# Attention and routing stage of an adaLN + mixture-of-experts block: statistics and normalised rows computed a step further ahead, one product moved to GpSimd, two extra matmuls per step

## The chip, the cores and the metric

One NeuronCore of a Trainium2 chip runs the whole program. The metric is the device time of one execution in microseconds (us); the median of three runs is quoted, and one further execution was profiled.

## The reference, cut to what matters

```python
# x: 16 batches x 512 tokens x 256; c: 16 x 256
mod = (silu(c) @ wmod).reshape(16, 6, 1, 256)           # sa, ca, ga, sb, cb, gb; ga, gb kept away from 0
h = layernorm(x) * (1 + ca) + sa
q, k, v = phi(h @ W_q), phi(h @ W_k), h @ W_v           # 64 wide, phi = elu + 1
o = causal linear attention: (sum_{s<=t} (q_t . k_s) v_s) / max(q_t . sum_{s<=t} k_s, 1e-6)
x = x + ga * (o @ W_o)
h = layernorm(x) * (1 + cb) + sb
logits = layernorm(h; rn_g, rn_b) @ router_w.T + router_b   # 8 experts, top 2, softmax
x = x + gb * sum over the 2 experts of weight * ffn_e(layernorm(h; ln_g[e], ln_b[e]))   # 256 -> 1024 -> 256, gelu
```

## The kernel before, in words

The program is written with an instruction stream per engine and semaphores between them; nothing reorders it. It has three parts. A short setup loads constants and computes `mod`. Then an attention and routing stage (to about 380 us) handles the 16 batches of 512 tokens. Last, an expert stage (380 us to the end) runs 71 tiles of up to 256 tokens through the expert networks. The change touches only the setup and the attention stage.

The attention stage is a software pipeline. `pipeline` calls `step(i, ...)` for i = 0 to 20 on every engine, and within one step the engines work on different batches, chosen by six flags: `project` (batch i, for i under 16), `attend` (batch i-1), `settle` (i-2), `norm` (i-3), `route` (i-4) and `place` (i-5). `r` is the parity of i. In one step:

- SP (the DMA queue) loads x two batches ahead (`load_x`, L366), stores finished rows, and loads the modulation rows `gaB` and `csB`. It also streams the expert weights in, which are split into two bf16 parts on the way.
- DVE (`step`, from L864 on) takes the mean and variance of the three layer norms: of x of batch i+1 (`stats(rows(i + 1), 0)`, bn_stats, L771), of the attention's result of batch i-2 (form 1), and of the modulated rows `h2` of batch i-3 (form 2). `moments` is L779, `var_eps` writes `ve` (L786).
- POOL turns `ve` into the inverse root `rs` with a power (`inverse_root`, L544), once a step for the three norms together, then DVE forms `nm` = -mean * rs (L803). `nm_s` counts them.
- ACT applies `rs` and `nm` (`normalise`, L628): to x at the start of the next step (`xc`), to the attention's result (`xn2`), and to `h2` (`nrm`).
- DVE modulates: `h2 = xn2 * csB` (L901), then `h2 += csB` (L908), both 128 partitions x 1024 elements.
- PE transposes `xc` (L1322), computes the scores of batch i-1 (L1334), the ranks of batch i-5 (L1341 to L1345), the projections of batch i (L1355 to L1358), the transposes of `nrm` (L1369), the product with k (L1381 to L1387), logits (L1398), the output projection (L1407) and transposes of k (L1414). In odd steps four matmuls for a bias (L1315) come first. The scores use the banks that the output projection filled, so they wait until DVE has added them to x (`x2`, L968).
- DVE forms phi(q), phi(k) (L926), running sums and the denominator (L930, L932), the low parts of the expert weights (L940 in odd steps, L946 in even ones), then `den`, the residual sum `x2` (L968), the choice of experts (`choose`, `dl`, `ix`, `oh`, `ohs`), and with PE's ranks the list positions `slot` (`cnt`, `pick`, `slotf`, L1046 to L1064).
- POOL forms `wog` (L559, 64 x 256), and sends each batch's 512 rows to the experts' lists by 8 indirect DMAs (L551), four before the power (`scatter(.., (0, 1))`, waiting for `slot`), four behind it.

```python
                if place:                                            # POOL, L560 on
                    ...
                    scatter(i - 5, 1 - r, (0, 1))
                if project or attend or norm:
                    inverse_root(i + 1, 1 - r)
                if place:
                    scatter(i - 5, 1 - r, (2, 3))
```

## Time and profile before

| | |
|---|---|
| median of 3 runs | 1125.11 us (1123.71 to 1125.61) |
| the profiled execution, its own time | 1125.48 us |
| its span, first to last instruction | 1123.6 us |
| mean granted TensorE clock | 0.922 of full |
| busy over the span: PE, DVE, ACT, POOL | 88%, 79%, 48%, 51% |
| in 140 to 300 us: PE, DVE, ACT, POOL (busy us of 160) | 131.2, 151.2, 128.4, 104.3 |
| granted clock, 100 to 300 us / 420 us to the end | 0.81 to 0.89 / 1.00 |

A row of the profile names an engine, a source line, an operation, what it writes and reads (out<-in by the program's names), and its times. "store" is a large buffer that holds x, weights and several tiles; "banks" is PSUM. A busy engine is one that executes; waiting and the issue of plain DMAs are not counted. In the stage to 380 us PE is not at its full clock all the time; in the expert stage it is.

### The profile page before, as it was taken

The page shows a single profiled execution, that of the slowest core. Times are in us where ns is not written, and L with a number is a line of the kernel's source. Part 1 is how long each engine was busy: PE and PEld are TensorE (multiplying, and loading weights), DVE is VectorE, ACT ScalarE, POOL GpSimd, SP SyncE. Part 2 cuts the span into 40 slices and gives each one's busy share as a digit, 9 for nine tenths or more (in the row PEclk, how much of TensorE's full clock was granted, in tenths as well). Part 3 has the DMA queues.
Part 4 walks back from the last instruction along what each step waited for, and adds up shares of the span by engine and source line. Part 5 has one row for each costly group of instructions (what it writes and reads, how often), then busy time and mean ns, then how long its engine had stood idle before and what let it go on. Part 6 is the DMA issues. An engine that isn't in the chain of part 4 may idle for free.

```text
span 1123.6 us, 31567 instructions
## 1 busy us (share of the span) xinstructions
PE 988.9 (88%) x8116; PEld 806.3 (72%) x8117; DVE 889.1 (79%) x3010; ACT 542.9 (48%) x1123; POOL 573.6 (51%) x478
## 2 busy tenths in 40 slices
PE   5777879887945099999999999999999999999997
PEld 1334545554534088888888888888888888888875
DVE  5578999999985567777877877877877877877776
ACT  1668787878843134434444443444443443444443
POOL 2121666666667536655455445445445445545543
PEclk8798888888965599999999999999999999999999
DMA  4465777876869466665565555566555556566453
GB/s 134 133 227 194 237 230 260 291 271 212 315 233 401 122 185 132 137 123 92 96 118 98 106 112 104 98 109 99 94 108 103 90 108 108 87 120 122 88 100 49
DMA packets 162626, 169.80 MB, mean 151 GB/s; under 512 B 89340, under 2 KB 136968, under 8 KB 158472
## 3 DMA queue, kind: packets, MB, share of 16 engines
q1 hardware_dynamic: 129736, 114.24, 36.5%
q0 software_dynamic: 32832, 54.88, 25.3%
q8 instruction: 25, 0.41, 0.2%
q14 instruction: 33, 0.27, 0.1%
HBM read 94.67 MB, written 62.78 MB: 140 GB/s over the span
## 4 chain that ended last, share of the span: by engine, by line
PE 66%; issue 8%; DVE 8%; POOL 6%; ACT 2%; DMA 1%; POOLq 0%; DVEq 0%; SPq 0%; ACTq 0%
PE banks L1440 32%; PE banks L1452 31%; POOL lists L551 5%; PE banks L1334 2%; DVE st L771 2%; POOL rs L544 2%; DVE store L968 1%; PE banks L1322 1%; ACT rowbuf L628 1%; DVE mv L779 1%; ACT store L712 1%; DVE rowbuf L908 1%; DMA out<-rowbuf,ydst 0%; DVE store L926 0%; DVE ix L1001 0%
## 5 line engine op out<-in xcount | busy, mean ns | idle before, releaser
L1440 PE MATMUL banks<-nhl,store 128*128 128x256 bf16 (+1 forms) x3408 | 450.5, 268 | 28.0 <-DMA nhl<-xhl 24.8
L740 ACT ACTIVATE gf<-banks,b1t 128x256 f32<-128x256 f32 (+1 forms) x568 | 263.0, 463 | 429.1 <-PE banks L1440 411.7
L1452 PE MATMUL banks<-store 128*128 x3240 | 448.0, 273 | 0.5
L1440 PEld LDWEIGHTS banks<-nhl,store 128*128 x3408 | 324.1, 98 | 71.0 <-issue 30.1
L587 POOL DMA_INDIRECT out<-rowbuf,ydst x135 | 223.7, 1657 | 294.1 <-DVE rowbuf L1222 222.0
L1452 PEld LDWEIGHTS banks<-store 128*128 128x128 bf16 x3240 | 310.5, 98 | 41.9 <-issue 1.8
L1231 DVE CAST store<-gf 128x256 bf16<-128x256 f32 (+1 forms) x568 | 180.5, 318 | 130.7 <-ACT gf L740 99.3
L1233 DVE TENSOR_TENSOR store<-gf,store 128x256 bf16<-128x256 f32 (+1 forms) x568 | 234.7, 413 | 19.5
L551 POOL DMA_INDIRECT lists<-store,slot x128 | 141.0, 1102 | 96.3 <-issue 49.0
L578 POOL DMA_INDIRECT store<-y_rows,ygb x135 | 135.2, 1001 | 63.3 <-issue 51.8
L544 POOL TENSOR_TENSOR rs<-ve,mhalf 128x12 f32<-128x12 f32 (+2 forms) x20 | 39.0, 1950 | 84.6 <-DVE ve L786 84.5
L628 ACT ACTIVATE rowbuf<-store,nm,rs 128x256 f32<-128x256 f32 x128 | 66.1, 588 | 23.5 <-DVE nm L803 23.3
L1222 DVE SCALAR_TENSOR_TENSOR rowbuf<-rowbuf,yw,store 128x256 f32<-128x256 f32 x135 | 59.4, 479 | 0.2 <-DVE rowbuf L1212 0.2
L1322 PE MATMUL banks<-ident,rowbuf 128*128 128x128 f32 x128 | 25.1, 360 | 31.8 <-ACT rowbuf L628 31.8
L1334 PE MATMUL banks<-store,vT 64*128 64x512 f32 (+3 forms) x128 | 38.4, 662 | 16.5 <-DVE store L968 8.5
L1183 DVE TENSOR_TENSOR xhl<-rowbuf,xhl 128x512 bf16<-128x512 f32 (+1 forms) x71 | 46.6, 658 | 7.7 <-ACT xhl L731 7.7
L731 ACT ACTIVATE xhl<-rowbuf 128x512 bf16<-128x512 f32 (+1 forms) x71 | 42.6, 600 | 18.4 <-DMA rowbuf<-lists 18.4
L1212 DVE TENSOR_TENSOR rowbuf<-banks,b2t 128x256 f32<-128x256 f32 x135 | 50.8, 416 | 0.7 <-PE banks L1452 0.7
L1322 PEld LDWEIGHTS banks<-ident,rowbuf 128*128 128x128 f32 x128 | 19.7, 183 | 41.1 <-ACT rowbuf L628 39.5
L771 DVE BATCH_NORM_STATS2 st<-store 128x6 f32<-128x256 f32 x128 | 44.8, 412 | 2.3 <-DMA store<-in_L_attn_x 2.0
L1355 PE MATMUL banks<-store,wqk 128*128 128x512 f32 x64 | 42.0, 790 | 3.0 <-ACT store L664 3.0
L1334 PEld LDWEIGHTS banks<-store,vT 64*128 64x128 f32 x128 | 23.2, 276 | 27.6 <-issue 24.5
(225 smaller groups left out, 970.0 us busy)
## 6 DMA issues: line engine op xcount, KB each, us to landing
rowbuf<-lists SPq DMA_DIRECT2D x64, 264.0 KB
store<-in_L_ffn_w SPq DMA_DIRECT2D x16, 1024.0 KB, 6.0
wsplit<-store SPq DMA_DIRECT2D x16, 1024.0 KB, 5.7
store<-wsplit SPq DMA_DIRECT2D x16, 1024.0 KB, 11.1
b2t<-in_L_ffn_b SPq DMA_DIRECT2D x71, 128.0 KB
store<-in_L_attn_x SPq DMA_DIRECT2D x16, 512.0 KB, 9.6
out<-store SPq DMA_DIRECT2D x16, 512.0 KB, 9.9
csB<-mod_rows SPq DMA_DIRECT2D x16, 256.0 KB, 4.0
```

What stands on the lines that cost most here:

```text
L544: g.tensor_tensor(rs[:, r, n, :], ve[:, n, :], mhalf[:, n, :], ALU.pow).then_inc(rs_s, 1)
L551: g.indirect_dma_start(list_d, bass.IndirectOffsetOnAxis(ap=slot[:, b % NR, t, c:c + 1], axis=0), nrm[:, b % NR, c, :], None).then_inc(sca ...
L578: g.indirect_dma_start(gbr[:, r, h, :], None, y_d[GBROW:GBROW + NB, :], bass.IndirectOffsetOnAxis(ap=ygb[:, r, h:h + 1], axis=0)).then_inc ...
L587: g.indirect_dma_start(out_rows, bass.IndirectOffsetOnAxis(ap=ydst[:, r, h:h + 1], axis=0), yt[:, r, h, :], None, compute_op=ALU.add).then ...
L628: last = a.activation(out(c), src(c), ACT.Identity, bias=nm[:, r, n, c:c + 1], scale=rs[:, r, n, c:c + 1])
L740: a.activation(gf[:, c % 2, 0:halves(j) * P], MM[c % 2][:, 0:halves(j) * P], ACT.Gelu, bias=b1t[:, r, c:c + 1]).then_inc(gf_s, 1)
L771: last = v.bn_stats(st[:, n, c, :], src(c))
L1231: v.tensor_copy(gh[:, c, cols], gf[:, c % 2, cols]).then_inc(gh_s, 1)
L1233: v.tensor_tensor(gl[:, c, cols], gf[:, c % 2, cols], gh[:, c, cols], ALU.subtract).then_inc(gl_s, 1)
L1334: last = t.matmul(SC[s], vT[at, q, s // 2 * P:(s // 2 + 1) * P], q_of[at, q, s * P:T], start=True, stop=True)
L1440: last = t.matmul(MM[c % 2][:, 0:halves(j) * P], w, nhl[:, r, m, 0:halves(j) * P], start=n == 0, stop=n == 5)
L1452: last = t.matmul(ACC[r][h][:, 0:D], g[:, c, h * P:(h + 1) * P], w, start=c == 0 and n == 0, stop=c == NI - 1 and n == 2)
```

## The change

In the attention stage, the statistics of x are taken for batch i+2 in step i (batch 0 and 1 before the first step), and ACT normalises batch i+1 near the end of step i (`centred`) where it used to normalise batch i at the start of step i. Power and `nm` are still formed once a step, with one more before the first step. SP loads x of batches 2 and 3 in step 0 and i+3 in step i. The product `xn2 * csB` is done by POOL, behind `wog` and ahead of the first four scatter DMAs; DVE adds to its result. PE runs two matmuls on the constants `ident` and `onesf` into the bank `Q` ahead of the projections, which overwrite it. The sum for the router's bias moves from the setup to the end of DVE's step 0.

```diff
@@ SP @@
             def load_x(i, half, r):
-                if isinstance(i, int):
-                    if i + 2 < NB:
-                        sp.wait_ge(got_x[r], 16 * (half + 1))
-                        sp.dma_start(resid[:, (i + 2) * NC:(i + 3) * NC, :], x_v[i + 2]).then_inc(got_x[r], 16)
...
+                for b in range(2 if i == 0 else i + 3, min(i + 4, NB)):
+                    sp.wait_ge(got_x[b % 2], 16 * (b // 2))
+                    sp.dma_start(resid[:, b * NC:(b + 1) * NC, :], x_v[b]).then_inc(got_x[b % 2], 16)
@@ POOL @@
+            inverse_root(-1, 1)
             inverse_root(0, 0)
...
+                if norm:
+                    b, q = i - 3, 1 - r
+                    pool.wait_ge(got_cs[q], 16 * (half if q == 0 else half - 1))
+                    pool.wait_ge(xn2_s, b + 1)
+                    wait_past(pool, nrm_s, b - 1)
+                    g.tensor_tensor(h2[q], xn2, csB[:, q, D:2 * D].unsqueeze(1).to_broadcast([P, NC, D]), ALU.mult).then_inc(h2m_s, 1)
                 if place:
@@ ACT @@
+            def centred(b, r):
+
+                act.wait_ge(got_x[b % 2], 16 * (b // 2) + 16)
+                wait_past(act, xT_s, b)
+                normalise(lambda c: xc[:, c, :], rows(b), r, 0, xc_s)
+
+            act.wait_ge(nm_s, 1)
+            centred(0, 1)
...
-                if project or norm or route:
-                    act.wait_ge(nm_s, i + 1)
-                if project:
-                    act.wait_ge(got_x[r], 16 * half + 16)
-                    wait_past(act, xT_s, i)
-                    normalise(lambda c: xc[:, c, :], rows(i), r, 0, xc_s)
...
+                if 0 < i < NB - 1:
+                    centred(i + 1, r)
                 if project:
                     act.wait_ge(phi_s, i + 1)
@@ DVE @@
-            var_eps(0, 1)
+            var_eps(-1, 1)
+            dve.wait_ge(got_x[1], 16)
+            dve.wait_ge(mv_s, 1)
+            hold(dve, "dve")
+            stats(rows(1), 0)
+            neg_mean_rstd(-1, 1)
+            dve.wait_ge(nm_s, 1)
+            dve.wait_ge(ve_s, 1)
+            moments(0, 1)
+            var_eps(0, 2)
...
-                if project and not (isinstance(i, int) and i == NB - 1):
-                    if r == 0:
-                        dve.wait_ge(got_x[1], 16 * half + 16)
-                    else:
-                        dve.wait_ge(got_x[0], 16 * half + 32)
+                if i + 2 < NB:
+                    dve.wait_ge(got_x[r], 16 * half + 32)
                     hold(dve, "dve")
-                    stats(rows(i + 1), 0)
+                    stats(rows(i + 2), 0)
                 if norm:
...
-                    v.tensor_tensor(h2[q], xn2, csB[:, q, D:2 * D].unsqueeze(1).to_broadcast([P, NC, D]), ALU.mult).then_inc(h2m_s, 1)
+                    dve.wait_ge(h2m_s, b + 1)
+                    hold(dve, "dve")
+                    v.tensor_tensor(h2[q], h2[q], csB[:, q, 0:D].unsqueeze(1).to_broadcast([P, NC, D]), ALU.add).then_inc(h2_s, 1)
@@ PE @@
                 if project:
-                    pe.wait_ge(hT_s, i + 1)
                     if r == 0:
                         wait_past(pe, phi_s, i)
                     else:
                         pe.wait_ge(b1r_s, half + 1)
+                    if i == 0:
+                        pe.wait_ge(modc_s, 1)
+                    for n in range(2):
+                        t.matmul(Q[:, :], ident[:, :], onesf[:, :], start=True, stop=True)
+                    pe.wait_ge(hT_s, i + 1)
                     wait_past(pe, ktok_s, i)
```

POOL, one full step of the attention stage (steps 6 to 15 all have this order). Before:

```order
L551 DMA lists<-store,slot 67840x264 x4
L559 TENSOR_TENSOR wog<-wo,gaB 64x256
L551 DMA lists<-store,slot 67840x264 x4
L544 TENSOR_TENSOR rs<-ve,mhalf 128x12
L551 DMA lists<-store,slot 67840x264 x4
```

The same step in the changed kernel:

```order
L548 DMA lists<-store,slot 67840x264 x4
L556 TENSOR_TENSOR wog<-wo,gaB 64x256
L562 TENSOR_TENSOR rowbuf<-rowbuf,csB 128x1024
L548 DMA lists<-store,slot 67840x264 x4
L540 TENSOR_TENSOR rs<-ve,mhalf 128x12
L548 DMA lists<-store,slot 67840x264 x4
```

The product of 128 x 1024 elements now stands ahead of the first four scatter DMAs, and so ahead of the power.

DVE, from the last setup instruction through step 0 to the first `nm` of it. Before:

```order
L858 TENSOR_TENSOR rbias<-rbias,banks 128x8 [waits base_set,got_r,rb_ps]
L861 COPY lge<-lngb 128x4 [waits setup_done]
L771 BN_STATS st<-store 128x6 [waits nm_s,got_x1]
...
L786 TENSOR_SCALAR ve<-mv 128x12 [waits mv_s]
L926 SCALAR_TENSOR_TENSOR store<-banks,ex 128x512 [waits ex_s]
```

The changed kernel there:

```order
L876 COPY lge<-lngb 128x4 [waits base_set]
L783 BN_STATS st<-store 128x6 [waits nm_s,got_x0]
...
L798 TENSOR_SCALAR ve<-mv 128x12 [waits mv_s]
L940 SCALAR_TENSOR_TENSOR store<-banks,ex 128x512 [waits ex_s]
...
L882 TENSOR_TENSOR rbias<-rbias,banks 128x8 [waits got_r,rb_ps]
```

The statistics ahead of the first phi (L926, now L940) are now those of batch 2, so they wait for the second load on `got_x0` and not for the first on `got_x1`.

## Rows read from the trace of the kernel before

**Rows 1.** Steps 13, 14: length, busy us of PE, PEld, DVE, ACT, POOL; then granted clock

```profile
259.09:278.18 19.09, 14.06 (x86) 9.88 (x86) 18.20 (x69) 15.64 (x32) 13.01 (x12) 0.86 0.74 228
278.18:297.14 18.96, 17.15 (x94) 10.03 (x94) 18.00 (x70) 14.53 (x30) 11.42 (x9) 0.82 0.89 341
```

**Rows 2.** Timeline of POOL: start us, us, what, [idle before <-releaser]

```profile
259.27 0.96 POOL L551 DMA_INDIRECT lists<-store,slot  x1 [0.30 <-issue]
260.25 0.74 POOL L559 TENSOR_TENSOR wog<-wo,gaB 64x256 f32<-64x256 f32 x1
264.43 1.00 POOL L551 DMA_INDIRECT lists<-store,slot  x1 [3.45 <-DVE slot L1064]
265.74 1.72 POOL L551 DMA_INDIRECT lists<-store,slot  x1 [0.30 <-issue]
...
269.16 0.96 POOL L551 DMA_INDIRECT lists<-store,slot  x1 [0.30 <-issue]
270.50 2.30 POOL L544 TENSOR_TENSOR rs<-ve,mhalf 128x12 f32<-128x12 f32 x1 [0.39 <-DVE ve L786]
...
277.84 0.74 POOL L559 TENSOR_TENSOR wog<-wo,gaB 64x256 f32<-64x256 f32 x1
```

**Rows 3.** Timeline of DVE in the same steps, and one row of ACT

```profile
260.41 0.64 DVE L1009 TENSOR_TENSOR ohs<-oh 128x32 bf16<-128x32 f32 x1
...
262.63 0.23 DVE L1052 TENSOR_TENSOR pick<-oh,cnt 128x64 f32<-128x64 f32 x1
...
263.42 0.17 DVE L1064 CAST slot<-slotf 128x8 int32<-128x8 f32 x1
...
265.41 1.21 DVE L901 TENSOR_TENSOR rowbuf<-rowbuf,csB 128x1024 f32<-128x1024 f32 x1
...
271.22 0.52 ACT L706 ACTIVATE store<-store 64x384 f32<-64x384 f32 x1 [2.81 <-DVE store L926]
...
273.09 0.17 DVE L803 SCALAR_TENSOR_TENSOR nm<-mv,rs 128x12 f32<-128x12 f32 x1
...
279.60 0.19 DVE L1009 TENSOR_TENSOR ohs<-oh 128x32 bf16<-128x32 f32 x1
...
281.77 0.19 DVE L1046 TENSOR_TENSOR cnt<-banks,base 128x32 f32<-128x32 f32 x1 [0.25 <-PE banks L1345]
```

**Rows 4.** Timeline of DVE and POOL in step 2, where `wog` meets two DVE instructions

```profile
64.05 1.22 DVE L930 TENSOR_TENSOR_SCAN zT<-onesf,store 64x512 f32<-64x512 f32 x1
64.64 1.16 POOL L559 TENSOR_TENSOR wog<-wo,gaB 64x256 f32<-64x256 f32 x1 [0.59 <-DMA gaB<-mod_rows]
65.31 1.04 DVE L932 TENSOR_TENSOR store<-store,zT 64x512 f32<-64x512 f32 x1
```

**Rows 5.** Timeline of steps 0 and 1; the landing is that of x's loads

```profile
26.30 0.58 SPq L368 DMA_DIRECT2D store<-in_L_attn_x  x1
DMA to landing us min/median/max: 8.7/9.0/9.2
32.44 0.68 DVE L926 SCALAR_TENSOR_TENSOR store<-banks,ex 128x512 f32<-128x512 f32 x1
33.82 3.58 PE L1315 MATMUL banks<-store,lge 128*1 128x512 f32 x8
39.90 2.92 PE L1334 MATMUL banks<-store,vT 64*128 64x512 f32 x8
```

**Rows 6.** Timeline of PE: projections at full clock and at half clock; scores at full clock

```profile
42.75 2.00 PE L1355 MATMUL banks<-store,wqk 128*128 128x512 f32 x4
...
110.81 3.76 PE L1355 MATMUL banks<-store,wqk 128*128 128x512 f32 x4
...
145.94 1.52 PE L1334 MATMUL banks<-store,vT 64*128 64x512 f32 x8 [1.11 <-issue]
```

**Rows 7.** Timeline of POOL in the drain: first and last of 32 scatter DMAs in a row

```profile
338.07 1.27 POOL L551 DMA_INDIRECT lists<-store,slot  x1 [3.59 <-DVE slot L1064]
...
381.59 0.96 POOL L551 DMA_INDIRECT lists<-store,slot  x1 [0.30 <-issue]
```

More of the change, by code:

```diff
@@ L535, in inverse_root @@
             def inverse_root(i, r):
-                pool.wait_ge(ve_s, i + 1)
-                wait_past(pool, xc_s, upto(i - 1))
+                pool.wait_ge(ve_s, i + 2)
+                wait_past(pool, xc_s, upto(i))
                 wait_past(pool, xn2_s, upto(i - 4))
                 wait_past(pool, nrm_s, upto(i - 5))
-                wait_past(pool, nm_s, i - 1)
+                wait_past(pool, nm_s, i)
                 n = used(i)
                 g.tensor_tensor(rs[:, r, n, :], ve[:, n, :], mhalf[:, n, :], ALU.pow).then_inc(rs_s, 1)
+            inverse_root(-1, 1)
             inverse_root(0, 0)
@@ L646, in step @@
                     a.activation(b1rows, Q[0:H + 1, :], ACT.Copy).then_inc(b1r_s, 1)
+                if i + 1 < NB or norm or route:
+                    act.wait_ge(nm_s, i + 2)
                 if norm:
@@ L666, in step @@
                     last.then_inc(hT_s, 1)
+                if i == 0:
+                    centred(1, 0)
                 if attend:
@@ L788, in stats_before @@
             def stats_before(i):
-                if not isinstance(i, int):
-                    return 3 * i - 4
-                return min(i + 1, NB) + min(max(i - 2, 0), NB) + min(max(i - 3, 0), NB)
+                return min(i + 2, NB) + min(max(i - 2, 0), NB) + min(max(i - 3, 0), NB)
             def neg_mean_rstd(i, r):
-                dve.wait_ge(rs_s, i + 1)
-                wait_past(dve, xc_s, upto(i - 1))
+                dve.wait_ge(rs_s, i + 2)
+                wait_past(dve, xc_s, upto(i))
                 wait_past(dve, xn2_s, upto(i - 4))
@@ L854, in _, with router_bias @@
             v.tensor_copy(ef[:, 0, 0:1], base[:, 0:1]).then_inc(base_set, 1)
-            dve.wait_ge(rb_ps, 1)
-            dve.wait_ge(got_r, 32)
             dve.wait_ge(base_set, 1)
-            v.tensor_tensor(rbias[:, :], rbias[:, :], S[1][:, 0:E], ALU.add).then_inc(setup_done, 1)
-            dve.wait_ge(setup_done, 1)
+            hold(dve, "dve")
             v.tensor_copy(lge[:, :], lngb[:, 0, :]).then_inc(lge_s, 1)
+            def router_bias():
+                dve.wait_ge(rb_ps, 1)
+                dve.wait_ge(got_r, 32)
+                v.tensor_tensor(rbias[:, :], rbias[:, :], S[1][:, 0:E], ALU.add).then_inc(setup_done, 1)
+                dve.wait_ge(setup_done, 1)
             def step(i, half, r, project, attend, settle, norm, route, place):
                 taken = stats_before(i)
-                dve.wait_ge(nm_s, i + 1 if not isinstance(i, int) else min(i + 1, NB + 4))
+                dve.wait_ge(nm_s, min(i + 2, NB + 5))
                 if settle:
@@ L897, in step @@
                     dve.wait_ge(got_cs[q], 16 * (half if q == 0 else half - 1))
-                    dve.wait_ge(xn2_s, b + 1)
-                    wait_past(dve, nrm_s, b - 1)
+                    dve.wait_ge(h2m_s, b + 1)
                     hold(dve, "dve")
-                    v.tensor_tensor(h2[q], xn2, csB[:, q, D:2 * D].unsqueeze(1).to_broadcast([P, NC, D]), ALU.mult).then_inc(h2m_s, 1)
-                if project and not (isinstance(i, int) and i == NB - 1):
+                    v.tensor_tensor(h2[q], h2[q], csB[:, q, 0:D].unsqueeze(1).to_broadcast([P, NC, D]), ALU.add).then_inc(h2_s, 1)
+                if i + 2 < NB:
                     moments(0, taken)
@@ L905, in step @@
                 if norm:
-                    b, q = i - 3, 1 - r
-                    dve.wait_ge(h2m_s, b + 1)
-                    v.tensor_tensor(h2[q], h2[q], csB[:, q, 0:D].unsqueeze(1).to_broadcast([P, NC, D]), ALU.add).then_inc(h2_s, 1)
                     dve.wait_ge(h2_s, i - 2)
@@ L932, in step @@
                     v.tensor_tensor(oz[H:2 * H, r, :], qk[0:H, r, :], zT[:, :], ALU.mult).then_inc(qz_s, 1)
+                if i == 0:
+                    router_bias()
                 if project or attend or norm:
@@ L1327, in step @@
                     pe.wait_ge(vT_s, b + 1)
+                    if b == 0:
+                        pe.wait_ge(setup_done, 1)
                     wait_past(pe, x2_s, b)
```

7 lines of the change are left out of this document (2 added, 5 removed).

## The prediction

> **What bounds the kernel now.** I read the page first (busy shares, the slices), then busy time by stretch, the chain of waits, and the timelines of POOL and DVE over two steps. The expert stage, two thirds of the time, is untouched: in the page's slices PE stands at 9 tenths or more there, at full clock. All that can change lies ahead of 385 us.
>
> There, a step takes 19 us; DVE is busy 18.2 and 18.0 us of 19, PE 14 and 17, POOL 13 and 11 [rows 1]. The reader should see DVE nearly full, and suspect it. But the timelines show a second loop of the same length, through POOL, although POOL is a third idle. From `slot` (written at 263.42 + 0.17 = 263.59) it takes 0.84 until the first scatter DMA, then four of them to 270.12, then a wait of 0.38 for DVE's `ve`, then the power to 272.80, and 0.29 later comes `nm` [rows 2, 3]. Behind `nm` DVE has the weights' low part, `den` and the residual sum, then choice and ranks, up to the next `slot`. So POOL's loop is shorter than DVE's by only about 0.38 us a step: that is all that DVE can gain before POOL bounds.
>
> The scatter loop is longer than four DMAs need: one takes 0.96 alone, but 1.72 where DVE's product L901 (265.41 to 266.62) lies over it [rows 2, 3]. And DVE waits for POOL too: `ohs` takes 0.64 at 260.41 and 0.19 at 279.60; the first began inside POOL's `wog` (260.25 to 260.99) and ended 0.06 behind it [rows 2, 3]. Other way round, `wog` took 1.16 in step 2 because DVE's running sum with two SBUF inputs held until 65.27; `wog` ended 0.53 after that, and the next DVE product took 1.04 [rows 4]. **An instruction of DVE with two SBUF inputs and a tensor product of POOL do not run side by side.** The Trainium skill (SBUF — State Buffer, Who interferes with whom) says that the second one blocks until the first ends; by that rule the trace agrees.
>
> **The change part by part.**
>
> *Product from DVE to POOL.* DVE loses 1.21 us in 13 steps (3 to 15) [rows 3]. POOL gains an instruction that the trace does not show. Its price from `wog`, 64 x 256 in 0.74 alone [rows 2], of which 0.53 came after the blocker [rows 4]: four times the columns give 4 x 0.53 = 2.1 to 4 x 0.74 = 3.0. I take 2.4, four times 0.53 and once the rest (0.21), rounded. The Trainium skill (GPSIMD Engine Reference, 3.1) gives about 2.6 cycles per element against 1 on DVE; at 1.2 GHz that would be 2.2 us, an estimate, and the sum would fall by some 2 us.
>
> Where does it run? POOL's idle stretch ahead of `slot` is 3.45 us [rows 2], so POOL itself has room. DVE has not: its two-input instructions `oh`, `ohs` and `pick`, all needed for `slot`, lie in that stretch. Step 13: `wog` ends at 260.99, the product runs 261.0 to 263.4, and `pick`, due at 262.63, waits 0.8. Step 14: `wog` 277.84 to 278.58, the product 278.6 to 281.0, over `oh` and `ohs`; `ohs` ends at 281.45 where it ended at 279.79 [rows 2, 3], 1.65 later, of which 0.25 was DVE waiting for ranks anyway; 1.4 remain. `slot` is late by 0.8 and 1.4, the 0.38 that POOL waited for `ve` is returned each time (the removed 1.21 makes `ve` early), so `nm` and the next step come 0.4 and 1.0 later. Sum 1.45, call it 1.5 a pair. Steps 6 to 15 are five pairs: **+7.5**. DVE's saved 1.21 becomes idle time ahead of `nm`.
>
> Steps 3 and 4 have no scatter; POOL is free, DVE or the scores bound: -1.2 each. Step 5 scatters for the first time: -1.2 and +0.7 for `dl` held up, **-2.9** together.
>
> *Drain.* From 338.07 POOL issues 32 scatter DMAs with hardly a gap until 381.59 + 0.96 [rows 7], and the expert stage waits for the last. Step 18's product (2.4 and 0.1 of gap) goes in front of four of them: +2.5. Step 17's fits the 3.59 idle ahead of 338.07 [rows 7] but holds `pick` for 0.6. Step 16 is like step 14, +1.6. **+4.7**.
>
> *Statistics further ahead.* In step 0 DVE now needs batch 2. Its load is issued at 26.30 and lands 8.7 to 9.2 us later, at 35.3 [rows 5]. Statistics (1.4), their aggregation and `ve` take until 37.6, so phi of batch 0 starts there and not at 32.44 [rows 5], 5.2 late. Behind it come PE's transposes of k (0.7), the bias matmuls (3.58 [rows 5]) and the transposes of `xc` (2.0); `xc` itself is there already, which saves 0.5. The first scores move from 39.90 [rows 5] by 4.7. In later steps the order frees nothing that anyone waits for: the scores wait for the residual sum, and PE's gap ahead of the transposes ends a few tenths before that. The extra statistics ahead of the first step lie in DVE's wait for the modulation matmuls (3.7 us idle). The loads of x are one further ahead and are not waited for again.
>
> *Two matmuls on constants.* They have the projections' shape: 2.00 us at full clock, 3.76 at half [rows 6]. From step 3 on phi (L926) waits for DVE's turn: ACT has finished `ex` and two copies of the output behind it (0.8), and then stands idle for 2.81 until phi comes [rows 3], a slack of some 3.5, so 2.0 is covered; if DVE came 1.5 sooner the cover would be gone. In steps 1 and 2 DVE waits for `ex`, so they lie on the path: 2.3 in step 1 (the clock is partly down), and 2.0 less 1.0 in step 2, where the projections now run at full clock. With the start: 4.7 + 2.3 + 1.0 = **+8.0**. In step 0 they lie under the wait for batch 2.
>
> The Trainium skill (TensorE: Matmul & The Clock Gate, What's actually happening) says that activity releases the throttle; by this rule the two matmuls would pay for themselves. The rows price it as the third rival.
>
> **Sum:** 8.0 - 2.9 + 7.5 + 4.7 = 17.3. On the profiled execution's own time, 1125.5, that is **1142.8 us**; this execution stands 0.4 above the median of the runs, which is less than their spread.
>
> **The rivals.**
>
> 1. *Faster.* POOL's product falls between DVE's two-input instructions, and with L901 gone the second scatter DMA takes 0.96 and not 1.72. Then POOL's loop is shorter by 0.38 + 0.76 = 1.14, about what DVE gains: -11.5 in ten steps, + 8.0 - 2.9 for the start, + 2.5 for step 18: 1121.6. It decides if `slot` is not late. For it: three two-input instructions there are short (0.2 each), and it is the order of arrival that counts. Against: `wog` ends where they begin, and DVE's sum L908 moves to where L901 was, over the same DMA.
> 2. *No harm, no gain.* `slot` is on time but the sum collides with the DMA as the product did: -0.38 x 10 + 5.1 + 2.5, 1129.3.
> 3. *The clock.* The granted clock is 0.86 and 0.82 here [rows 1]. If the added matmuls hold it at its 2.4 GHz level, scores take 1.52 and not 2.9 [rows 5, 6], the bias matmuls half, and the start loses some 7 us less: 1136. In steps 6 to 15 earlier ranks don't help while `ohs` is late. Against: PE is idle for several us while the first phi waits.
> 4. *PE bounds.* At half clock 3.76 us on top of 14 and 17 leave nothing of 19 [rows 1]: steps near 20.5, some 15 us more than now in ten, with start and drain 1157. The gaps of PE in a step (some 4 us) speak against it.
>
> That the change does not do what it says I leave out: order and waits show each part.
>
> **How the numbers follow.** Forecast 0.52, rival 1 0.20, rival 2 0.12, rival 3 0.10, rival 4 0.06. No change means within 0.2% (2.3 us), about what a measurement of this kernel can tell. Rival 1 is faster: 0.20. Rival 2 is just above the bound, a third of it within: 0.04 same. The rest, 0.76, slower. The product's price between 2.1 and 3.0 moves the forecast from 1139 to 1150; the two matmuls at 3.76 in steps 1 and 2 add 3. The range takes in all of rivals 2 and 3 and most of 1 and 4: 1119 to 1157.
>
> **What would show it.** In the profile after: POOL's product of about 2.4 us right behind `wog`; `ohs` in even steps and `pick` in odd ones stretched until it ends; `slot` at 5.3 to 6.2 us behind the residual sum's end where it was 4.5 to 4.8; `nm` led by idle time of DVE that POOL's power ends; steps of 19.7; phi of batch 0 at 37.6; 2.5 us more between first and last scatter of the drain. I am wrong if the step is shorter than 18.6 with DVE's `ohs` and `pick` at 0.2, if the first phi is at 33, or if the second scatter DMA after `slot` has fallen to 0.96.

## The result and the profile after

The changed kernel takes 1161.57 us (median; 1158.27 to 1162.31) against 1125.14: a ratio of 1.0316 [1.0291, 1.0342], 3.2% slower. One further run of it, at 3348.22 us, was disturbed and is left out. The forecast, 1142.8 us, had the direction but less than half of the size: +17.3 where +36.4 came, and the time lies outside the range, 4.6 us above its upper end.

The profiled execution took 1158.27 us, span 1155.8; it is the fastest of the runs, so the places below add up to some 32 us of the 36. Steps 13 and 14 (between ends of the residual sum, as in [rows 1]: length, busy us of PE, PEld, DVE, ACT, POOL, then the granted clock):

```profile
277.24:299.38 22.14, 18.18 (x90) 11.27 (x90) 19.61 (x67) 14.50 (x30) 15.84 (x13) 0.77 0.59 182
299.38:319.00 19.62, 15.68 (x98) 9.53 (x98) 17.03 (x61) 15.95 (x33) 12.98 (x9) 1.00 0.82 316
```

Two steps take 41.76 us where they took 38.05 [rows 1]; DVE's busy time in them rose from 36.20 to 36.64 although 1.21 us of work a step was taken from it. Busy time that grows when work is removed is time in which an instruction is held. The table follows the end of the residual sum from step to step in both timelines, in us; the last row is the start of the last scatter DMA plus 0.96.

| part | before | after | more | forecast |
|---|---|---|---|---|
| to the end of step 2 | 70.7 | 74.7 | 4.0 | 8.0 |
| steps 3 to 5 | 55.9 | 55.0 | -0.9 | -2.9 |
| steps 6 to 15 | 189.0 | 211.4 | 22.4 | 7.5 |
| step 16 | 17.7 | 19.6 | 1.8 | 1.6 |
| from there to the last scatter | 49.2 | 54.2 | 5.0 | 3.1 |

So two thirds of the loss lie in steps 6 to 15, 2.24 us a step instead of 0.75, and so does the error of 15 us; those of the other rows cancel. POOL's timeline after, which answers to [rows 2] (start, us, what, [idle before <-releaser]):

```profile
255.87 0.73 POOL L556 TENSOR_TENSOR wog<-wo,gaB 64x256 f32<-64x256 f32 x1
256.55 2.35 POOL L562 TENSOR_TENSOR rowbuf<-rowbuf,csB 128x1024 f32<-128x1024 f32 x1
263.75 0.99 POOL L548 DMA_INDIRECT lists<-store,slot  x1 [4.86 <-DVE slot L1080]
265.05 1.74 POOL L548 DMA_INDIRECT lists<-store,slot  x1 [0.30 <-issue]
...
269.33 3.06 POOL L540 TENSOR_TENSOR rs<-ve,mhalf 128x12 f32<-128x12 f32 x1
...
278.39 0.74 POOL L556 TENSOR_TENSOR wog<-wo,gaB 64x256 f32<-64x256 f32 x1
279.08 2.35 POOL L562 TENSOR_TENSOR rowbuf<-rowbuf,csB 128x1024 f32<-128x1024 f32 x1
```

The product is where it was said to be and costs what was said: 2.35 us. What was not said stands on DVE (the rows that answer to [rows 3]):

```profile
255.78 3.15 DVE L1015 TENSOR_TENSOR dl<-mx 128x4 f32<-128x4 f32 x1
...
262.74 0.17 DVE L1080 CAST slot<-slotf 128x8 int32<-128x8 f32 x1
...
264.74 1.21 DVE L918 TENSOR_TENSOR rowbuf<-rowbuf,csB 128x1024 f32<-128x1024 f32 x1
...
269.07 1.22 DVE L944 TENSOR_TENSOR_SCAN zT<-onesf,store 64x512 f32<-64x512 f32 x1
...
272.57 0.22 DVE L813 SCALAR_TENSOR_TENSOR nm<-mv,rs 128x12 f32<-128x12 f32 x1 [1.56 <-POOL rs L540]
...
277.15 0.15 DVE L1015 TENSOR_TENSOR dl<-mx 128x4 f32<-128x4 f32 x1
...
278.04 3.48 DVE L1022 TENSOR_TENSOR oh<-experts,ix 128x64 f32<-128x64 f32 x1 [0.18 <-DVE ix L1017]
281.56 0.19 DVE L1025 TENSOR_TENSOR ohs<-oh 128x32 bf16<-128x32 f32 x1
```

`dl`, 128 x 4 elements and 0.15 us alone, takes 3.15 us: from 255.78 until POOL's product ends at 258.90. One step on it is `oh` (0.22 alone, 3.48 here), held by the last scatter DMA, by `wog` and by the product, to 281.43. In both cases the instruction was already waiting while `wog` ran, `wog` ended, and the product got the turn. `slot` ends 7.05 us behind the residual sum in one step (262.91 against 255.86) and 7.13 in the next. These are two of the longest holds; in the ten steps it is 5.7 to 7.2 where it was 4.2 to 5.0. Where the product came later behind `wog`, the same `oh` was held by the last scatter DMA alone, and got in ahead of `wog` (195.20 to 195.93), as it does before the change (0.48 at 259.89):

```profile
194.84 0.47 DVE L1022 TENSOR_TENSOR oh<-experts,ix 128x64 f32<-128x64 f32 x1 [0.18 <-DVE ix L1017]
```

```profile
196.49 2.36 POOL L562 TENSOR_TENSOR rowbuf<-rowbuf,csB 128x1024 f32<-128x1024 f32 x1 [0.56 <-issue]
```

Each step can be cut at `slot`, power and `nm`. Summed over steps 6 to 15, in us, read from both timelines:

| stretch | before | after | more | forecast |
|---|---|---|---|---|
| end of the residual sum to end of `slot` | 46.6 | 66.6 | 20.0 | 11.0 |
| to the start of the power | 68.7 | 64.8 | -3.9 | -3.8 |
| the power | 23.1 | 24.8 | 1.7 | 0 |
| its end to the end of `nm` | 4.8 | 5.2 | 0.4 | 0 |
| end of `nm` to the end of the residual sum | 45.9 | 50.2 | 4.3 | 0 |

So `slot` is late by 2.0 us a step on average, and another 6.4 us in all come behind it.

PE answers to `ohs` and pays twice, since its clock falls meanwhile to the 1.2 GHz level: the ranks wait for `ohs`, and the matmuls on constants (L1372) run at 3.76.

```profile
281.81 0.21 PE L1358 MATMUL banks<-ohs,before 128*128 128x32 bf16 x1 [2.83 <-DVE ohs L1025]
282.04 3.76 PE L1372 MATMUL banks<-onesf,ident 128*128 128x512 f32 x4
```

```profile
290.95 0.69 DVE L940 SCALAR_TENSOR_TENSOR store<-banks,ex 128x512 f32<-128x512 f32 x1 [1.11 <-ACT ex L698]
```

There phi waits 1.11 us for `ex`, and `den` 0.85 for the multiplication by `wog`: the cover that I had given the constants from step 3 on is gone in this step. It is gone in the four steps in which the constants take 3.76 (7, 10, 13 and 15), where `nm` to residual sum takes 5.6 to 6.0 us and not 4.4 to 4.7; these are the 4.3 of the table.

The start, answering to [rows 5]: the load of batch 2 is waited for, phi of batch 0 comes at 37.45 (forecast 37.6), the bias matmuls take 3.33 and the first scores start at 43.16 (forecast 44.6). The clock was up by then, so `xc`'s transposes took 1.09 and not 2.0.

```profile
35.29 1.41 DVE L783 BATCH_NORM_STATS2 st<-store 128x6 f32<-128x256 f32 x4 [10.46 <-DMA store<-in_L_attn_x]
37.45 0.69 DVE L940 SCALAR_TENSOR_TENSOR store<-banks,ex 128x512 f32<-128x512 f32 x1
38.88 3.33 PE L1330 MATMUL banks<-store,lge 128*1 128x512 f32 x8
43.16 1.55 PE L1351 MATMUL banks<-store,vT 64*128 64x512 f32 x8
44.64 1.98 PE L1372 MATMUL banks<-onesf,ident 128*128 128x512 f32 x4
```

The drain, answering to [rows 7]: its first scatter waits for a `slot` that is 2.7 us later behind the last residual sum than before (368.09 - 360.7 against 338.07 - 333.4; forecast 0.6), and step 18's product is in the row (forecast +2.5; from first scatter to last 46.78 us against 44.48, so +2.3).

```profile
368.09 1.23 POOL L548 DMA_INDIRECT lists<-store,slot  x1 [4.68 <-DVE slot L1080]
...
379.88 2.37 POOL L562 TENSOR_TENSOR rowbuf<-rowbuf,csB 128x1024 f32<-128x1024 f32 x1
...
413.91 0.96 POOL L548 DMA_INDIRECT lists<-store,slot  x1 [0.30 <-issue]
```

### The profile page after: what moved, and what is told of

It reads as the page before. It is cut to its first block, busy times and chain, and to the rows that moved or that the text cites. A ratio compares the mean times of both kernels' runs of the same rounds, so it can differ in the third digit from the quotient of the medians.

```text
span 1155.8 us, 31692 instructions
## 1 busy us (share of the span) xinstructions
PE 1013.0 (88%) x8180; PEld 816.7 (71%) x8181; DVE 899.5 (78%) x2996; ACT 542.9 (47%) x1123; POOL 613.5 (53%) x495
## 4 chain that ended last, share of the span: by engine, by line
PE 61%; POOL 2%; issue 2%; DMA 1%; DVE 1%; ACT 0%; SPq 0%; POOLq 0%; DVEq 0%; ACTq 0%
PE banks L1461 31%; PE banks L1473 30%; POOL lists L548 2%; DMA nhl<-xhl 1%; DMA rowbuf<-lists 0%; POOL rs L540 0%; DMA lists<-store,slot 0%; ACT gf L752 0%; POOLq L60 0%; POOL rowbuf L562 0%; SPq L449 0%; DVE store L1247 0%; DVE rowbuf L1228 0%; DVE xhl L1199 0%; DVE rowbuf L1238 0%
## 5 line engine op out<-in xcount | busy, mean ns | idle before, releaser
L1249 DVE TENSOR_TENSOR store<-gf,store 128x256 bf16<-128x256 f32 (+1 forms) x568 | 234.6, 413 | 19.6
L540 POOL TENSOR_TENSOR rs<-ve,mhalf 128x12 f32<-128x12 f32 (+2 forms) x21 | 42.4, 2020 | 68.7 <-DVE ve L798 68.4
L1351 PE MATMUL banks<-store,vT 64*128 64x512 f32 (+3 forms) x128 | 31.3, 550 | 35.0 <-DVE store L984 28.5
L562 POOL TENSOR_TENSOR rowbuf<-rowbuf,csB 128x1024 f32<-128x1024 f32 x16 | 37.7, 2354 | 23.0 <-issue 12.6
L1351 PEld LDWEIGHTS banks<-store,vT 64*128 64x128 f32 x128 | 18.9, 224 | 42.5 <-issue 39.4
L1372 PE MATMUL banks<-onesf,ident 128*128 128x512 f32 x64 | 44.9, 839 | 0.0
L1419 PEld LDWEIGHTS banks<-rTg,store 128*128 128x128 f32 x256 | 36.3, 226 | 10.9 <-issue 10.9
```

The costliest lines, as they stand in the source:

```text
L1249: v.tensor_tensor(gl[:, c, cols], gf[:, c % 2, cols], gh[:, c, cols], ALU.subtract).then_inc(gl_s, 1)
L1351: last = t.matmul(SC[s], vT[at, q, s // 2 * P:(s // 2 + 1) * P], q_of[at, q, s * P:T], start=True, stop=True)
```

## The experiments

In the expectations, "step n took" means the time between two ends of the residual sum. All ratios are against the kernel before, measured beside the run.

**Which part of the change costs.** Five kernels take the change apart. `only_product` is the kernel before with the product on POOL; `only_constants` has only the matmuls in front of the projections; `only_ahead` only the statistics and rows further ahead; `undo_product` is the changed kernel with the product back on DVE; `undo_constants` is the changed kernel without the matmuls. What moves in and out (the rest of the change is `only_ahead`):

```diff
@@ POOL, in or out @@
+                if norm:
...
+                    pool.wait_ge(xn2_s, b + 1)
...
+                    g.tensor_tensor(h2[q], xn2, csB[:, q, D:2 * D]..., ALU.mult).then_inc(h2m_s, 1)
@@ DVE, out or in @@
-                    v.tensor_tensor(h2[q], xn2, csB[:, q, D:2 * D]..., ALU.mult).then_inc(h2m_s, 1)
@@ PE, in or out @@
+                    for n in range(2):
+                        t.matmul(Q[:, :], ident[:, :], onesf[:, :], start=True, stop=True)
```

> The kernel before, with the product xn2 * csB alone moved to POOL (statistics and constants as before). Theory A (DVE's instructions with two SBUF inputs wait for POOL's wog and product together, 3.1 to 3.5 us a step, and slot and all behind it come late): about 1.8 us more in each of steps 6 to 15, 5 more in the drain, 3 less in steps 3 to 5, so 1145 to 1150 against 1125. Theory B (the two matmuls on constants make the steps long, as phi waits for ex and den for the output projection): this kernel has none of them, so at most 5 us over before, from the drain.

> The kernel before, with only the two matmuls on constants ahead of the projections. Theory A: they lie under the wait of phi for DVE's turn from step 3 on, and cost 2 us each in steps 1 and 2: 1128 to 1130. Theory B: about 2 us in every step that has projections, 1145 or more. If they hold TensorE's clock at its upper level and that pays, below 1125.

> The changed kernel with the product back on DVE and without the matmuls on constants: only the statistics and the normalised rows further ahead. Phi of batch 0 starts near 37.5 us and not 32.4, as in the changed kernel, the first scores some 3 to 4 us later, the later steps stay at 18.9: 1127 to 1130 by both theories. A theory C, that the new order of ACT and DVE itself makes steps longer, would give steps of over 19.5 and 1135 or more.

> The changed kernel with the product back on DVE; statistics ahead and constants stay. Theory A: the cost of the two other parts alone, 1130 to 1134, steps near 19. Theory B: nearly all of the loss stays, 1150 or more.

> The changed kernel without the two matmuls on constants; product on POOL and statistics ahead stay. The three parts alone cost 23.5 (product), 3.9 (constants) and 5.6 us (ahead), 33 in sum, and the whole 36.4. If the constants' cover is gone once the product delays slot and projections (phi waits for ex, den for the output projection), taking them away gives back more than their 3.9: 1150 to 1155. If they are still covered: 1157 to 1160.

| kernel | median us | ratio | residual sum of step 5 / 15 / 16 ends at |
|---|---|---|---|
| before | 1125.1 | | 126.6 / 315.6 / 333.4 |
| only_product | 1148.65 | 1.0208 [1.0187, 1.0229] | 121.2 / 331.1 / 351.0 |
| only_constants | 1129.00 | 1.0036 [1.0024, 1.0048] | 126.9 / 316.6 / 337.0 |
| only_ahead | 1130.68 | 1.0046 [1.0033, 1.0060] | 130.6 / 318.7 / 339.1 |
| undo_product | 1129.84 | 1.0040 [1.0025, 1.0054] | 131.5 / 317.8 / 338.2 |
| undo_constants | 1156.61 | 1.0274 [1.0254, 1.0293] | 126.2 / 339.6 / 360.2 |
| after | 1161.57 | 1.0316 [1.0291, 1.0342] | 129.7 / 341.1 / 360.7 |

Of the first four kernels, each came out within 1 us of what theory A gave, and none as theory B or C had it. The product alone costs 23.5 us, and taking it out of the change gives 31.7 of the 36.4 back. In `only_product` steps 6 to 15 take 21.0 us, and every second `oh` is held as in the changed kernel, through `wog` (185.15) and the product behind it:

```profile
184.81 3.48 DVE L1007 TENSOR_TENSOR oh<-experts,ix 128x64 f32<-128x64 f32 x1 [0.18 <-DVE ix L1002]
```

```profile
185.15 0.74 POOL L559 TENSOR_TENSOR wog<-wo,gaB 64x256 f32<-64x256 f32 x1
185.84 2.35 POOL L565 TENSOR_TENSOR rowbuf<-rowbuf,csB 128x1024 f32<-128x1024 f32 x1
```

The other `oh`, in the even steps, starts 0.13 us after the product has (164.17 against 164.04) and takes 2.33, to the product's end. There `slot` comes 6.1 to 6.5 us behind the residual sum, and 7.1 where `oh` is held for 3.48.

The start and the constants without the product cost 4.7 us, and none of it in steps 6 to 15 (`undo_product`: 186.2 against 189.0). What the constants cost inside the whole change is 5.0 by the medians, between the two expectations, and those intervals touch. In the ten steps of `undo_constants` the stretch from `nm` to the residual sum is back at 45.5 us, so that the constants did cost their 4.7 there; but `slot` comes later still, 71.1 us in sum against 66.6, since `dl` or `oh` now meets `wog` and the product together in every step. The net is -2.0 for the constants in the ten steps and +3.5 by step 5. The starts are less certain than the ten steps: two profiled executions whose code is the same up to step 15 (`early_x2` and `early_x2_step16` below) differ by 2.9 us at the first residual sum.

**Is it POOL's time, or its reading?** `only_memsets` leaves the product on DVE and gives POOL, behind `wog`, four memsets of a buffer that no one uses at the time. They occupy POOL as long as the product does (2.28 us) but read nothing.

```diff
+                if norm:
+                    pool.wait_ge(xn2_s, i - 2)
+                    for n in range(4):
...
+                        g.memset(gf[:, :, :], 0.0).then_inc(blank_s, 1)
```

> The kernel before, product still on DVE, and POOL writes a constant into a tile not in use, four memsets of 512 columns, about 2.3 us, where the changed kernel has its product (behind wog, after xn2, ahead of the scatter DMAs). It reads no SBUF. Theory A (DVE is held by POOL's reading product): steps stay at 18.9, oh and dl are not held longer than by wog; only the drain grows by 2 to 5 us: 1127 to 1131. Theory D (POOL's own time is what is missing, whatever it does there): as only_product, 1145 or more.

1127.00 us, ratio 1.0019 [1.0009, 1.0028]; steps 6 to 15 take 18.9 us as before. The rows:

```profile
259.09 0.73 POOL L559 TENSOR_TENSOR wog<-wo,gaB 64x256 f32<-64x256 f32 x1
259.76 2.28 POOL L564 MEMSET gf<- 128x512 f32 x4
```

```profile
258.74 0.47 DVE L1011 TENSOR_TENSOR oh<-experts,ix 128x64 f32<-128x64 f32 x1 [0.18 <-DVE ix L1006]
259.25 0.64 DVE L1014 TENSOR_TENSOR ohs<-oh 128x32 bf16<-128x32 f32 x1
259.81 0.51 DVE L1018 CAST store<-ix 128x4 f32<-128x4 uint32 x1
...
261.47 0.23 DVE L1057 TENSOR_TENSOR pick<-oh,cnt 128x64 f32<-128x64 f32 x1
```

`ohs` is held by `wog` alone, to 259.89 as in [rows 3], and no two-input instruction by the memsets: `pick`, under them, takes its 0.23. So POOL's queue has room for 2.3 us, and what costs is that the product reads SBUF. A cast of DVE (0.17 alone) took 0.51 beside the memsets. The Trainium skill (SBUF — State Buffer, Who interferes with whom) has both halves: two SBUF inputs contend with POOL's reads and not with its writes, while casts can enter a mode that contends; the trace agrees.

**Does DVE get in between shorter pieces?** `four_pieces` is the changed kernel with the product in four instructions of 256 columns.

```diff
-                    g.tensor_tensor(h2[q], xn2, csB[:, q, D:2 * D]..., ALU.mult).then_inc(h2m_s, 1)
+                    for c in range(NC):
+                        last = g.tensor_tensor(h2[q][:, c, :], xn2[:, c, :], csB[:, q, D:2 * D], ALU.mult)
+                    last.then_inc(h2m_s, 1)
```

> The changed kernel with POOL's product cut into four instructions of 256 columns. If a waiting instruction of DVE gets in between two of POOL's, dl or oh wait for wog or one piece at most (0.8 us) and the steps lose 1 us or more: 1145 to 1152. If DVE is held until POOL's queue has no further reading instruction at hand, nothing is gained, and four overheads of 0.2 us are added: 1162 to 1170.

1157.76 us, ratio 1.0296 [1.0277, 1.0315]: between the two expectations, and not clear of the change itself, whose interval it overlaps.

```profile
153.20 0.74 POOL L556 TENSOR_TENSOR wog<-wo,gaB 64x256 f32<-64x256 f32 x1
153.89 2.77 POOL L563 TENSOR_TENSOR rowbuf<-rowbuf,csB 128x256 f32<-128x256 f32 x4
```

```profile
152.82 3.24 DVE L1024 TENSOR_TENSOR oh<-experts,ix 128x64 f32<-128x64 f32 x1 [0.18 <-DVE ix L1019]
156.10 0.61 DVE L1027 TENSOR_TENSOR ohs<-oh 128x32 bf16<-128x32 f32 x1
```

The pieces end near 154.6, 155.3, 156.0 and 156.66. `oh` waits through `wog` and three of them and comes at 156.06; `ohs` then waits for the fourth. So POOL's next instruction takes its turn ahead of DVE's waiting one three times in a row, and then it does not: the fourth piece follows the third as closely as the others do, and `oh` ends while it runs. Nor does a `wog` that follows at once keep `oh` out where the product is not ready behind it (the row at 194.84). How the chip gives the turn is not shown, and "POOL's next one always goes first" is not the rule. What the rows at 3.15, 3.48, 3.48 and 3.24 us show is that the order of asking does not decide either, and that with `wog` and the product back to back the waiting instruction gets no turn between them.

**Can a wait more make it faster?** If the lock is the cost, the product should run when DVE is at something else. `product_after_ohs` is the changed kernel with one more wait on POOL; `product_after_scatters` moves the product behind the step's first scatters; `only_product_after_ohs` puts the same wait into `only_product`.

```diff
                     wait_past(pool, nrm_s, b - 1)
+                    if place:
+                        pool.wait_ge(ohs_s, i - 4)
                     g.tensor_tensor(h2[q], xn2, csB[:, q, D:2 * D]..., ALU.mult).then_inc(h2m_s, 1)
@@ product_after_scatters: the product's block moved here @@
                     scatter(i - 5, 1 - r, (0, 1))
+                if norm:
...
+                    g.tensor_tensor(h2[q], xn2, csB[:, q, D:2 * D]..., ALU.mult).then_inc(h2m_s, 1)
                 if project or attend or norm:
                     inverse_root(i + 1, 1 - r)
```

> The changed kernel, but POOL's product also waits for `ohs`, so that only wog (0.74 us) can run beside `oh`. A wait is added and nothing is taken away. Theory A (what costs is that DVE's waiting two-input instruction gets no turn between wog and product, so that `oh` is held for 3.48 us and `ohs`, the ranks on PE, the clock and `slot` are all late): `oh` falls to some 0.8 us every second step; the product, 2.35 us, then holds `cnt`, `d` or `pick` for at most 1.5 us, `slot` comes 5.3 to 6.0 us behind the residual sum, steps 6 to 15 take 19.7 to 20.3 us instead of 21.1: 1144 to 1153 us in all against 1161.6. Rival B (POOL's time is what counts: product, scatters and power in one queue): the product starts some 1.5 us later, POOL's power with it, and the steps take 21.1 us or more: 1161 us or above. Rival C (any place of the product costs DVE its full 2.35 us): the hold only moves, 1158 to 1162.

> The changed kernel, but POOL issues the product behind the first two scatters of the step, so behind `slot`, where of DVE's instructions only the strips' mask (128 x 512, two inputs) and the add of the modulation are left before the logits. Theory A: dl, `oh`, `ohs`, cnt and pick are free of it, `slot` comes 4.5 to 5.3 us behind the residual sum; what it costs is the add, which now waits for the product (some 2.4 us from `slot`, where DVE has 1.4 us of statistics to do), and the power behind it: 1 to 1.5 us a step, steps of 19.9 to 20.4 us, 1145 to 1153 us. Rival B (POOL's queue counts): product and power both late, steps of 21 us and more, 1160 us or above.

> The kernel before with nothing but the product on POOL, and there with the wait for `ohs`. Without that wait it took 1148.65 us. Theory A (what the move of the product costs is the lock of `oh` and `dl` across wog and product; put behind `ohs`, the product costs DVE 0.7 to 1.3 us at `d` every second step and as much or less in the other, and takes 1.2 us away): steps 6 to 15 take 18.9 to 19.3 us, 1125 to 1132 us in all, so the work moved off DVE gains nothing even there. Rival B (DVE bounds the steps, and the 1.2 us taken from it come back once the lock is gone): steps of 18.0 to 18.6 us, 1115 to 1122 us. Rival C (POOL's queue, later by the product and the wait, sets the step through power and nm): 19.6 us and more, above 1134 us.

With the wait, the change takes 1138.96 us, ratio 1.0126 [1.0107, 1.0144]: 22.6 us less by an added wait, more than I had expected (1144 to 1153). Steps 7 to 15 take 19.3 us.

```profile
267.32 0.49 DVE L1024 TENSOR_TENSOR oh<-experts,ix 128x64 f32<-128x64 f32 x1 [0.18 <-DVE ix L1019]
267.85 0.65 DVE L1027 TENSOR_TENSOR ohs<-oh 128x32 bf16<-128x32 f32 x1
...
269.97 1.52 DVE L1046 TENSOR_SCALAR d<-dex 128x4 f32<-128x4 f32 x1
```

```profile
269.11 2.36 POOL L564 TENSOR_TENSOR rowbuf<-rowbuf,csB 128x1024 f32<-128x1024 f32 x1 [0.68 <-ACT rowbuf L633]
...
278.80 3.04 POOL L540 TENSOR_TENSOR rs<-ve,mhalf 128x12 f32<-128x12 f32 x1
```

`oh` and `ohs` meet `wog` alone, and what stays is `d`, held for 1.4 us until the product ends. In the next step nothing of this chain is held. `slot` comes 52.0 us in sum behind the residual sum in steps 6 to 15 (66.6 in the changed kernel, 46.6 before). `product_after_scatters` took 1201.56 us, ratio 1.0684 [1.0666, 1.0702], far above theory A; the number is rival B's, late product and late power. I had overlooked that the step's first scatters are four DMAs, 1.28 us apart. The product starts 5.7 us behind `slot`, and DVE's add stands waiting for it:

```profile
289.39 2.36 POOL L567 TENSOR_TENSOR rowbuf<-rowbuf,csB 128x1024 f32<-128x1024 f32 x1
```

```profile
291.88 1.23 DVE L918 TENSOR_TENSOR rowbuf<-rowbuf,csB 128x1024 f32<-128x1024 f32 x1 [6.26 <-issue]
```

Steps of 23.9 us, then: add, statistics, power and `nm` follow the product in one chain. On the lock its time says nothing, but its `slot` does: with the product out of the way it comes 46.6 us in sum behind the residual sum in the ten steps, as before the change.

`only_product_after_ohs` took 1133.34 us, ratio 1.0065 [1.0051, 1.0078], against 1148.65 without the wait. The time is above what theory A gave (1125 to 1132) and just under rival C's 1134. Most of the loss was the lock; but steps 7 to 15 still take 19.6 us and not 18.9 (theory A: 18.9 to 19.3). The rest is `d`, and a second thing that the rows show:

```profile
263.82 0.17 DVE L1067 CAST slot<-slotf 128x8 int32<-128x8 f32 x1
...
270.15 1.22 DVE L933 TENSOR_TENSOR_SCAN zT<-onesf,store 64x512 f32<-64x512 f32 x1
```

```profile
266.14 1.72 POOL L551 DMA_INDIRECT lists<-store,slot  x1 [0.30 <-issue]
...
270.44 3.03 POOL L544 TENSOR_TENSOR rs<-ve,mhalf 128x12 f32<-128x12 f32 x1
```

POOL's power starts 6.45 us behind `slot`; before it was 6.91 (270.50 - 263.59 [rows 2, 3]). These 0.46 us are all that DVE's saved 1.21 brings POOL's loop. But 0.29 ahead of the power DVE has started its running sum, and the power takes 3.03 instead of 2.30. So 0.46 is gained and 0.73 lost; and the second scatter DMA still takes 1.72, under the add instead of the product. That a running sum just ahead lengthens the power stands in the kernel before too: in step 16 a power of 8 columns takes 2.36 us there (308.22) behind a running sum that began 0.33 earlier (307.88), and 1.67 in step 17 (326.82).

**What comes of the rest of the change.** `early_x2` keeps the statistics ahead, leaves the product on DVE and the constants out, and loads batches 2 and 3 in the setup, so that step 0 has no load to wait for. `early_x2_step16` adds seven matmuls on constants in step 16 alone.

```diff
@@ SP, setup @@
+            for b in range(2, 4):
+                sp.wait_ge(got_x[b % 2], 16)
+                sp.dma_start(resid[:, b * NC:(b + 1) * NC, :], x_v[b]).then_inc(got_x[b % 2], 16)
@@ PE, early_x2_step16: n in range(4) ahead of step 16's scores, n in range(3) behind its ranks @@
+                if isinstance(i, int) and i == NB:
+                    pe.wait_ge(phi_s, NB)
+                    for n in range(4):
+                        t.matmul(Q[:, :], ident[:, :], onesf[:, :], start=True, stop=True)
```

> Only the statistics ahead (as only_ahead), and the loads of batches 2 and 3 issued in the setup, behind the small loads, and not behind 2 MB of expert weights. The prediction put the start's loss on this landing. If so, phi of batch 0 comes when ex is there, near 28 us and not 38, the first scores near 34 instead of 44.6: 10 us less than only_ahead at the first scores, 1120 to 1123 in all, faster than before. If another wait takes its place there, 1128 or more.

> The kernel with the loads of batches 2 and 3 in the setup, statistics ahead, the product on DVE and no constants in the steps (1121.8 us), and in step 16 alone seven matmuls on constants into the bank that no one uses then: four in front of the scores, three behind the ranks. Theory A (step 16 takes 20.4 us instead of 17.8 there because the granted clock is half from 304 us on, so that scores, transposes, logits and the multiplications by wog take 2.9, 2.0, 3.6 and 3.8 us): with them the clock stays up, logits 1.95, wog's 1.98, step 16 17.8 to 18.2 us, and 2.2 to 2.8 us less in all: 1119.0 to 1119.7 us. Rival B (step 16 is set by DVE, and the clock only goes along): owo's duration falls but the step stays 20.2 to 20.6 us and the time 1121.8. Rival C: the matmuls come in the way of the scores and cost 1 us: 1122.5 to 1123.

`early_x2` took 1121.80 us, ratio 0.9974 [0.9963, 0.9985]: faster than before by 3.3 us, and by 8.9 than `only_ahead`, which differs in the place of two loads. Phi of batch 0 comes at 27.4 and the first scores at 32.5. The sum of step 15 ends 9.8 us earlier than before, at 305.8; but step 16 takes 20.4 us where it took 17.7. `early_x2_step16` took 1117.36 us, ratio 0.9938 [0.9922, 0.9953], 4.4 less again (expected 2.2 to 2.8). Step 16 (length, busy us, granted clock) in the kernel before, `early_x2` and `early_x2_step16`:

```profile
315.60:333.40 17.80, 11.13 (x64) 8.62 (x64) 13.41 (x57) 7.49 (x17) 10.98 (x10) 0.69 0.72 265
```

```profile
304.10:326.20 22.10, 14.68 (x64) 11.42 (x64) 15.14 (x62) 7.49 (x17) 13.30 (x12) 0.50 0.73 268
```

```profile
306.76:325.30 18.54, 12.09 (x70) 8.06 (x70) 14.94 (x62) 7.49 (x17) 12.31 (x11) 0.87 0.72 270
```

(The last two windows begin 1.7 us earlier than the first, with the residual sum that ends step 15.) And PE's multiplication by `wog`, for which `den` waits:

```profile
328.11 1.98 PE L1407 MATMUL banks<-wog,store 128*128 128x257 f32 x8
```

```profile
320.00 3.77 PE L1425 MATMUL banks<-wog,store 128*128 128x257 f32 x8
```

```profile
318.73 1.98 PE L1432 MATMUL banks<-wog,store 128*128 128x257 f32 x8
```

With the added matmuls the clock is back at the 2.4 GHz level for transposes, logits and this one, and step 16 takes 16.8 us, 3.5 less than in `early_x2`. That is what the traces show of the 4.4; the rest is not traced to a cause, as the second execution started 2.9 us later and lost less behind step 16. This is what rival 3 was about, in the one step where it pays. The Trainium skill (TensorE: Matmul & The Clock Gate, What's actually happening) says that activity releases the throttle; by this rule the trace agrees. It also corrects the readings above: in `only_constants`, `only_ahead` and `undo_product` step 16 took 20.4 us as well, at a granted clock of 0.50 and with 3.8 us for this multiplication, so 2.7 of their 3.9, 5.6 and 4.7 us are neither start nor the constants' own time, but this clock. The same 20.4 stand in `product_after_ohs` and `only_product_after_ohs`: 2.7 of the 13.9 and 8.0 us that they are still slower than before.

## Why the prediction was right and wrong

**Direction, and the place, right.** The timelines showed before the change that two SBUF inputs on DVE and a product on POOL exclude each other [rows 3, 4], that `ohs` and `pick` stand on the way to `slot`, and that `slot` drives POOL's loop. The lock is the cause of the larger part: with reading replaced by writing it is gone (`only_memsets`), and with one wait that orders the two engines 22.6 us come back.

**The price of the product, right.** 2.35 us from four times a quarter (forecast 2.4).

**The hold, wrong: this is the step that failed.** "`slot` is late by 0.8 and 1.4" came from laying POOL's 2.4 us beside DVE's instructions where they stood, as if whoever asks first were next. For step 13 I let `ohs` pass when `wog` ended and had only `pick` held. The rows that would have shown a queue of two POOL instructions are not in the trace of before: there `wog` is followed by nothing that reads. In fact an instruction of DVE that waits during `wog` waits for the product too, when the product follows at once: 3.15 at `dl`, 3.48 at `oh`. Step 14's reading was right where the product met `oh` alone: `slot` at 6.1 to 6.5 us behind the residual sum in the even steps of `only_product` (forecast 6.2), but at 7.1 in the odd ones (5.3). In the changed kernel `slot` came 20.0 us later in the ten steps, where 0.8 and 1.4 a pair make 11.0. That `dl` has two inputs I had seen only for step 5. The 3.8 that I had taken off for `ve` came back (3.9). The rest of the error, 6.4 us, lies in two terms that I had put at nothing: the power that grows longer and the cover that is lost, the next two paragraphs.

**The 0.38 that POOL waited for `ve`, wrong in effect.** It was returned (0.46), and taken again where the power now starts under the running sum (+0.75, in four of the ten steps; two shorter powers at the end leave +1.7 in sum). I had asked what a removed instruction makes early, but not what the early one then meets.

**The cover of the constants, half right.** "From step 3 on covered" held in `only_constants` (+1.0 in all to step 15). In the changed kernel PE waits up to 2.84 us for `ohs`, the clock falls, the constants take up to 3.76 and phi waits for `ex` (1.11), 4.3 us in the ten steps: the cover depended on ranks that come early. (Two of them took 3.76 and 3.48 in `only_constants` as well, and stayed covered.)

**The start, half the size.** Phi at 37.45 as forecast; but +4.0 by step 2 and not 8.0. The clock was up: transposes 1.09 (2.0 forecast), so the first scores at +3.3; then the scores 1.55 where they took 2.92 [rows 5], which pays for most of the constants' 1.98 behind them, and the projections start at +3.7 (46.46 against 42.75 [rows 6]). But the added matmuls are not what kept the clock up here, as rival 3 had it: in `undo_constants`, without them, the same transposes take 1.09 and the same scores 1.55. What I had mis-sized is the clock at which PE works behind the first phi.

**Steps 3 to 5: -0.9, forecast -2.9.** Steps 3 and 4 gave -1.3 and -0.7 (forecast -1.2 each). In step 5, where I had `dl` held for 0.7, it took 0.15; `d` was held for 1.5 under the product, and the power took 3.05 under the running sum: +1.1 instead of -0.5.

**Drain.** Step 18's product +2.3 (2.5). Step 17 +2.7 (0.6), by the same failed step: its `dl` waits through the whole product (2.85). Step 16's +1.8 is near the forecast 1.6 by luck: its `slot` is only 1.1 late, the granted clock is 0.53 and the multiplication by `wog` takes 3.77 instead of 1.98, as in `only_constants` and `only_ahead`.

**The range** was made from the product's price (2.1 to 3.0 us) and the rivals. It held no term for the unknown rule of who comes next, though both readings could be priced from the rows. Held to the end of the product (263.4), step 13's `oh` makes `slot` late by 2.6 instead of 0.8; with step 14's 1.4 and twice 0.38 off that is an estimate of 3.2 a pair and 16.2 in ten steps. The measured hold less what came back is 16.1 (20.0 - 3.9). It would have put this case at 1142.8 - 7.5 + 16.2 = 1151.5, still short of the measured time by the two terms above and the later drain. Rival 4's number, 1157, came near, but not by its mechanism: with the constants alone the steps take 19.0 us, and PE delays four of the ten only once the hold has made the ranks late.

## What to carry to other kernels

Work moved from DVE to POOL is not paid for in POOL's time but in what it holds: look for DVE instructions with two SBUF inputs, however small, between its start and its end, and price each as held until the last of the reading instructions that POOL has ready in a row; that is an upper bound, since some got in earlier. Where the product must be on POOL, order it behind the last small instruction that the loop waits for; a wait that delayed the product by well under 1 us a step gave 22.6 us back. When an instruction is removed, follow the one that comes early to what it meets. When an instruction is held, ask which engine idles meanwhile, and which work counted as covered rests on it. And when a load becomes needed one step sooner, issue it one step sooner.

## What the runs showed of the hardware that I had not expected

- A DVE instruction with two SBUF inputs that waits for POOL was not served between `wog` and the product where the product followed at once (3.15 and 3.48 us), nor between `wog` and the first three of four pieces (3.24); it was served ahead of the fourth piece, and ahead of a `wog` with no product at once behind it (0.47).
- The lock reaches a small instruction with one SBUF input as well: `d`, a `tensor_scalar` of 128 x 4, took 1.52 instead of 0.16 under the product, and casts 0.51 instead of 0.17 beside memsets that read nothing.
- POOL's power of 12 columns took 3.03 to 3.06 us instead of 2.30 when DVE's running sum had started 0.26 to 0.30 us before it, and up to 3.31 in `product_after_ohs`, where the running sum started 0.01 before.
- The granted clock around step 16 (0.50 over 304 to 326 us in one kernel, 0.69 over the step in the kernel before) goes with 2.7 us in step 16, and seven matmuls on constants there took 3.5 us off it (4.4 by the medians), with no other change of the work.
